# Rows of the targets' terms by 32x32 transposes on VectorE behind one small product, and edge counts in 16 bits

## The reference

```python
h = (x @ W).reshape(n, H, C)
alpha_s = jnp.einsum('nhc,hc->nh', h, a_s)
alpha_d = jnp.einsum('nhc,hc->nh', h, a_d)
e = jax.nn.leaky_relu(alpha_s[src] + alpha_d[dst], 0.2)
m = jax.ops.segment_max(e, dst, num_segments=n)
e = jnp.exp(e - m[dst])
denom = jax.ops.segment_sum(e, dst, num_segments=n)
alpha = e / (denom[dst] + 1e-16)
out = jax.ops.segment_sum(h[src] * alpha[:, :, None], dst, num_segments=n)
...
out = layernorm(x + gat(elu(gat(x, 8 heads) + b1), 1 head) + b2)
```

## Time and profile before

| | us |
|---|---|
| median of 3 runs | 641.88 (641.84 to 642.15) |
| profiled execution | 641.79 |
| its span | 640.0 |
| TensorE busy | 632.6 |
| VectorE busy | 529.6 |
| ScalarE busy | 336.3 |
| GpSimd busy | 208.1 |

### The profile page before, as it was taken

One profiled execution on the slowest core, in us unless ns is written; L12 is line 12 of the kernel. 1 busy time (PEld: TensorE's weight loads), 2 busy tenths in 40 slices (PEclk: granted clock), 3 DMA queues, 4 the chain that ended last, 5 costly groups with the idle time before them and its releaser, 6 DMA issues.

```text
span 640.0 us, 9306 instructions
## 1 busy us (share of the span) xinstructions
PE 632.6 (99%) x3426; PEld 543.9 (85%) x3426; DVE 529.6 (83%) x928; ACT 336.3 (53%) x570; POOL 208.1 (33%) x122
## 2 busy tenths in 40 slices
PE   9999999999999999999999999999999999999996
PEld 5766568989888898989899988999898989887885
DVE  8999997889989878758684858797689868789876
ACT  7899982546524645444353635363455344534382
POOL 1000000140743824067404940375207540451230
PEclk9999999999999999999999999999999999999999
DMA  8422503125144323042302520270307130500002
GB/s 317 161 75 75 160 15 99 50 54 194 51 147 146 127 99 99 1 153 95 100 1 72 175 59 16 75 227 23 97 20 237 65 100 5 192 26 1 1 2 99
DMA packets 22173, 59.36 MB, mean 93 GB/s; under 512 B 2544, under 2 KB 2800, under 8 KB 22128
## 3 DMA queue, kind: packets, MB, share of 16 engines
q1 hardware_dynamic: 21984, 58.69, 28.2%
q10 hardware_dynamic: 144, 0.07, 0.0%
HBM read 54.03 MB, written 4.72 MB: 92 GB/s over the span
## 4 chain that ended last, share of the span: by engine, by line
PE 89%; DVE 9%; issue 0%; ACT 0%; DMA 0%; ACTq 0%
PE O L1289 31%; PE R L1184 9%; PE R L1190 9%; PE R L1187 9%; PE R L1256 6%; PE R L1262 6%; PE R L1259 6%; DVE ohd L709 3%; PE O L1201 3%; DVE ohs L713 2%; PE R L1206 1%; DVE junk L749 1%; PE O L1256 1%; PE O L1262 1%; PE O L1259 1%; PE O L1434 1%
## 5 line engine op out<-in xcount | busy, mean ns | idle before, releaser
L1111 POOL TENSOR_TENSOR W2l<-Wr,W2h 128x768 fp32r<-128x768 f32 x48 | 92.6, 1948 | 126.1 <-ACT W2h L425 126.1
L1184 PE MATMUL R<-W1h,xTh 128*128 128x384 f32 x312 | 106.3, 341 | 0.0
L1115 POOL TENSOR_TENSOR Pl<-L,Ph 128x512 fp32r<-128x512 f32 x34 | 55.5, 1651 | 153.8 <-ACT Ph L474 153.6
L1187 PE MATMUL R<-W1l,xTh 128*128 128x384 f32 x312 | 105.4, 338 | 0.0
L1190 PE MATMUL R<-W1h,xTl 128*128 128x384 f32 x312 | 105.4, 338 | 0.0
L1105 POOL TENSOR_TENSOR W1l<-Wr,W1h 128x768 fp32r<-128x768 f32 x30 | 58.8, 1970 | 129.3 <-ACT W1h L414 128.9
L749 DVE CUSTOM_DVE_ANT_0 junk<-h,abc 128x768 bf16<-128x768 f32 x64 | 64.0, 999 | 27.8 <-ACT h L437 26.7
L1289 PE MATMUL O<-W2h,gh 128*128 128x256 f32 (+1 forms) x384 | 78.5, 339 | 0.0
L1289 PE MATMUL O<-W2h,gl 128*128 128x256 f32 (+1 forms) x384 | 77.4, 336 | 0.0
L1289 PE MATMUL O<-W2l,gh 128*128 128x256 f32 (+1 forms) x384 | 77.4, 336 | 0.0
L1256 PE MATMUL R<-Ph,hh 128*128 128x512 f32 x168 | 66.3, 395 | 0.0
(11 more groups left out here) (186 smaller groups left out, 1186.2 us busy)
## 6 DMA issues: line engine op xcount, KB each, us to landing
Wr<-in_W SPq DMA_DIRECT2D x101, 384.0 KB, 3.6
abc<-in_as SPq DMA_DIRECT2D x9, 384.0 KB, 5.5
abc<-in_ad SPq DMA_DIRECT2D x9, 384.0 KB, 5.3
h_rows<-h SPq DMA_DIRECT2D x8, 384.0 KB, 2.4
hl<-h_rows SPq DMA_DIRECT2D x8, 384.0 KB, 6.0
xin<-in_xT SPq DMA_DIRECT2D x6, 256.0 KB, 5.8
xr<-in_x SPq DMA_DIRECT2D x1, 1536.0 KB, 6.7
out<-res SPq DMA_DIRECT2D x4, 384.0 KB, 2.3
```

The lines of the kernel that those rows point to most:

```text
L1111: e.tensor_tensor(W2l[:, m % N2, :], Wr[:, n, :], W2h[:, m % N2, :].bitcast(f32), ALU.subtract).then_inc(s_w2l, 1)
L1115: e.tensor_tensor(Pl[:, t, d0:d1], L[:, t, d0:d1], Ph[:, t, d0:d1].bitcast(f32), ALU.subtract).then_inc(s_Pl, 1)
L1184: e.matmul(bank[:, 0:HALF], xTh[:, f, xs], hi[:, ws], start=f == 0, stop=False)
L1187: e.matmul(bank[:, 0:HALF], xTh[:, f, xs], lo[:, ws], start=False, stop=False)
```

## The change

In heads 1 to 6 the two rows of the targets' terms are no longer made by eight transposes on TensorE. `terms` (VectorE) spreads the four columns of each quantity over 16 columns, masked by `quad` so that a partition keeps only the column of its own quarter. `columns` (TensorE) multiplies both (128 x 32) by `four`, which is one wherever two partitions agree modulo 32; each partition then has the 16 values of the partitions with its own number modulo 32. `rows` (VectorE) turns them by 32x32 transposes of a broadcast input into 512 columns: first `row2` in SBUF, for ScalarE, then the bank `r1`, for its own L814. The ring's use `r2` becomes `x`, released by `rows`. Heads 0 and 7 and the second layer keep the eight transposes. `terms(2)` moves from behind `maxima(2)` to behind `scale_A(1, 0)`. GpSimd builds `four` and `quad` at the start. `CT` becomes u16 in place of f32.

```diff
@@ RING
-    RING += [("r2", 2, 0), ("r1", 2, 0)]
+    RING += [("x", 2, 0), ("r1", 2, 0)]
...
-            RING += [("B", h, n) for n in range(4, 8)] + [("as", h, 0), ("r2", h, 0), ("r1", h, 0)]
+            RING += [("B", h, n) for n in range(4, 8)] + [("as", h, 0), ("x" if h < H - 1 else "r2", h, 0), ("r1", h, 0)]
...
-        CT = sb("CT", [128, NT, N], f32)
+        CT = sb("CT", [128, NT, N], u16)
...
+            if kind == "x":
+                return s_row, 2 * h
@@ ScalarE, scores
-                            e.wait_ge(s_bc, bc)
+                            if 0 < h < H - 1:
+                                e.wait_ge(s_row, 2 * h - 1)
+                            else:
+                                e.wait_ge(s_bc, bc_value(h, 1))
@@ VectorE, terms
+                if turned:
+                    if h == 1:
+                        e.wait_ge(s_four, 11)
+                    e.tensor_tensor(adm[:, :, :], by_b(ad), by_t, ALU.mult).then_inc(s_adm, 1)
                 e.wait_ge(s_amx, NT * h + hi)
                 e.tensor_tensor(zm[:, lo:hi], amx[:, lo:hi], ad, ALU.add).then_inc(s_zm, 1)
                 e.wait_ge(s_zm, n // 2 + 1)
+                if turned:
+                    e.tensor_tensor(zmm[:, :, :], by_b(zm[:, :]), by_t, ALU.mult).then_inc(s_zmm, 1)
+                    e.wait_ge(s_zmm, h)
+                    e.scalar_tensor_tensor(
+                        out=mcm[:, :, :], in0=zmm[:, :, :], scalar=SLOPE, in1=zmm[:, :, :], op0=ALU.mult, op1=ALU.max).then_inc(s_mc, 1)
+                    e.wait_ge(s_mc, h + 1)
+                    e.wait_ge(s_adm, h)
+                    e.tensor_tensor(rm[:, 0, :, :], adm[:, :, :], mcm[:, :, :], ALU.subtract).then_inc(s_r12, 1)
+                    e.scalar_tensor_tensor(
+                        out=rm[:, 1, :, :], in0=adm[:, :, :], scalar=SLOPE, in1=mcm[:, :, :], op0=ALU.mult, op1=ALU.subtract).then_inc(s_r12, 1)
+                    return
@@ VectorE, rows (called first thing in scores, heads 1 to 6)
+                cols = ring_bank("x", h, 0)[:, 0:2 * NT * 4].rearrange("p (i c) -> p i c", i=2)
+                e.wait_ge(s_bc, bc_value(h, 1))
+                if h > 1:
+                    e.wait_ge(s_L, NT * h)
+                e.transpose(row2[:, :].rearrange("p (c j) -> p c j", j=32), cols[:, 1, :].unsqueeze(2).broadcast_to([128, NT * 4, 32])).then_inc(s_row, 1)
+                if h == 1:
+                    e.wait_ge(s_y, 2)
+                else:
+                    e.wait_ge(*released(RING[RING_AT["r1", h, 0] - 2]))
+                e.transpose(ring_bank("r1", h, 0)[:, :].rearrange("p (c j) -> p c j", j=32), cols[:, 0, :].unsqueeze(2).broadcast_to([128, NT * 4, 32])).then_inc(s_row, 1)
@@ VectorE, order
                     maxima(h, 0, NT, ring_bank("as", h, 0))
+                    terms(h, 0, NT)
...
                     for i, k in enumerate(V_SCORES.get(h, ())):
                         products_W2(k, 0 if i else 8 * h + 8)
-                    scores(h, h, 0, NT, ring_bank("r1", h, 0), 3 * h + 3)
+                    scores(h, h, 0, NT, ring_bank("r1", h, 0))
...
                     scale_A(h, c)
+                    if h == 1 and c == 0:
+                        terms(2, 0, NT)
@@ GpSimd
+            e.tensor_tensor(four[:, 0:32], idn[:, 0:32], idn[:, 32:64], ALU.add).then_inc(s_four, 1)
+            e.tensor_tensor(four[:, 32:64], idn[:, 64:96], idn[:, 96:128], ALU.add).then_inc(s_four, 1)
+            e.wait_ge(s_four, 2)
+            e.tensor_tensor(four[:, 64:96], four[:, 0:32], four[:, 32:64], ALU.add).then_inc(s_four, 1)
+            e.wait_ge(s_four, 3)
+            for q in (0, 1, 3):
+                e.tensor_copy(four[:, 32 * q:32 * q + 32], four[:, 64:96]).then_inc(s_four, 1)
+            e.memset(quad[:, :], 0.0).then_inc(s_four, 1)
+            e.wait_ge(s_four, 7)
+            for b in range(4):
+                e.memset(quad[32 * b:32 * b + 32, b:b + 1], 1.0).then_inc(s_four, 1)
@@ TensorE
+            def columns(h, bank):
+                e.wait_ge(s_r12, 2 * h + 2)
+                if h == 1:
+                    e.wait_ge(s_four, 6)
+                e.matmul(bank[:, 0:2 * NT * 4], four[:, :], rm[:, :, :, :].rearrange("p i t b -> p (i t b)"), start=True, stop=True).then_inc(s_bc, 1)
...
-                            e.wait_ge(*((s_y, 5), (s_y, 3), (s_y, 4), (s_y, 6), (s_L, 2 * NT), (s_lk, 2 * NT))[n])
+                            e.wait_ge(*((s_y, 5), (s_y, 3), (s_y, 4), (s_y, 6), (s_row, 2), (s_lk, 2 * NT))[n])
...
-                    e.wait_ge(s_y, 2)
-                    targets(1, 0, NT, (ring_bank("r2", 1, 0), ring_bank("r1", 1, 0)), 4)
+                    e.wait_ge(s_y, 1)
+                    columns(1, ring_bank("x", 1, 0))
...
-                    if c == (0 if h == 2 else 1 if h == H - 1 else 2) and h > 1:
+                    if c == 1 and h == H - 1:
                         targets(h, 0, NT, (None, None), 2 * h + 2)
+                    elif 1 < h < H - 1 and c == (0 if h == 2 else 2):
+                        columns(h, take("x", h, 0))
```

More of the change, by code:

```diff
@@ L79, in gat_resnorm_kernel @@
         xTl = sb("xTl", [128, FT, N], f32r)
-        CT = sb("CT", [128, NT, N], f32)
+        CT = sb("CT", [128, NT, N], u16)
+        row2 = sb("row2", [128, N], f32)
+        four = sb("four", [128, 128], f32)
+        quad = sb("quad", [128, 4], f32)
+        adm = sb("adm", [128, NT, 4], f32)
+        zmm = sb("zmm", [128, NT, 4], f32)
+        mcm = sb("mcm", [128, NT, 4], f32)
+        rm = sb("rm", [128, 2, NT, 4], f32)
+        sb("pad1", [128, 300], f32)
         with ExitStack() as c4:
@@ L207, in gat_resnorm_kernel @@
         s_dh, s_dl = sem("s_dh"), sem("s_dl")
+        s_four, s_adm, s_zmm, s_row = sem("s_four"), sem("s_adm"), sem("s_zmm"), sem("s_row")
         s_A, s_y, s_ex, s_em, s_g, s_gh, s_gl, s_C = (
@@ L216, in oh_value, with bc_value @@
             return (s_ohsa, ACT_J.index(j) + 1) if on_act(j) else (s_ohsd, DVE_J.index(j) + 1)
+        def bc_value(h, i):
+            return 1 + i if h == 0 else 2 * h + 2 + i if h < H - 1 else 2 * H + 3 * (h - H + 1) + i
         def Pl_value(h, t):
@@ L451, in scaled_as, with scores @@
                 e.mul(as02[:, :], asd[:, h % 2, 0, :], SLOPE).then_inc(s_as02, 1)
-            def scores(h, n, lo, hi, b2k, free, bc, between=None):
+            def scores(h, n, lo, hi, b2k, free, between=None):
                 d0, d1 = 128 * lo, 128 * hi
@@ L549, in head_2 @@
                     evict_B(2, 0, u // 2 - 1)
-            scores(0, 0, 0, NT, ring_bank("r2", 0, 0), (), 2, head_2)
+            scores(0, 0, 0, NT, ring_bank("r2", 0, 0), (), head_2)
             evict_B(2, 1, 0)
@@ L562, in head_2 @@
                             evict_B(2, 3, u // 2 - 1)
-                    scores(1, 1, 0, NT, ring_bank("r2", 1, 0), (gl_value(0, FT - 1), (s_g, FT)), 5, head_2)
+                    scores(1, 1, 0, NT, row2, (gl_value(0, FT - 1), (s_g, FT)), head_2)
                     high_sums(1)
@@ L576, in scalar_program @@
                     scaled_as(2, 24)
-                    scores(2, 2, 0, NT, ring_bank("r2", 2, 0), (gl_value(1, FT - 1), (s_g, 2 * FT)), 8, lambda u: high_w1(3, 3 + u) if u in (1, 2) else None)
+                    scores(2, 2, 0, NT, row2, (gl_value(1, FT - 1), (s_g, 2 * FT)), lambda u: high_w1(3, 3 + u) if u in (1, 2) else None)
                     high_h(2, 0)
@@ L603, in scalar_program @@
                     high_w2(h - 1, 5)
-                    scores(h, h, 0, NT, ring_bank("r2", h, 0), (gl_value(h - 1, FT - 1), (s_g, FT * h)), 3 * h + 2,
+                    scores(h, h, 0, NT, row2 if h < H - 1 else ring_bank("r2", h, 0), (gl_value(h - 1, FT - 1), (s_g, FT * h)),
                            lambda u, h=h: high_w1(h + 1, 1 + u) if h + 1 < H and 1 <= u <= 4 else None)
@@ L680, in scalar_program @@
             scaled_as(H, 65)
-            scores(H, H, 0, NT, ring_bank("r2", H, 0), (gl_value(H - 1, FT - 1), (s_g, FT * H)), 26, first_h2)
+            scores(H, H, 0, NT, ring_bank("r2", H, 0), (gl_value(H - 1, FT - 1), (s_g, FT * H)), first_h2)
             part_h2(2, 1, 3)
@@ L796, in maxima, with terms @@
                         accum_out=amx[:, t:t + 1]).then_inc(s_amx, 1)
+            def terms(h, lo, hi):
+                par = h % 2
+                ad = asd[:, par, 1, lo:hi]
+                n = 2 * h if h < H else 2 * H + lo
+                turned = 0 < h < H - 1
+                by_t, by_b = quad[:, :].unsqueeze(1).broadcast_to([128, NT, 4]), (lambda a: a.unsqueeze(2).broadcast_to([128, NT, 4]))
+                if turned:
+                    if h == 1:
+                        e.wait_ge(s_four, 11)
+                    e.tensor_tensor(adm[:, :, :], by_b(ad), by_t, ALU.mult).then_inc(s_adm, 1)
                 e.wait_ge(s_amx, NT * h + hi)
@@ L805, in maxima, with rows, scores @@
                     out=r12[:, 1, lo:hi], in0=ad, scalar=SLOPE, in1=mc[:, lo:hi], op0=ALU.mult, op1=ALU.subtract).then_inc(s_r12, 1)
-            def scores(h, n, lo, hi, b1k, bc):
```

(22 more changed lines are left out.)

8 lines of the change are left out of this document (3 added, 5 removed).

## The result

The kernel after takes 644.22 us (median, 643.89 to 647.19, 10 runs) where the kernel before took 641.98 beside it (641.74 to 642.20, 10 runs): ratio 1.0045, 95% interval 1.0033 to 1.0057. It is slower, by 2.24 us, where 2.3 were forecast.

A forecast was written before the change was run, and what follows sets the result against it. TensorE was taken to bound the kernel (busy 632.6 of 640.0 us), VectorE only from 20 to 80 us. -5.27 + 0.9 + 0.3 + 1.15 + 0.26 + 5.0 = +2.3 on 641.79 gave 644.1 us; range 640.0 to 648.5.

The forecast's parts named there:

- case (b): Rival: same stalls but milder, 3.0 us in heads 5 and 6, 0.3 in head 1; 640.7, no change; chance 0.20.
- Removed and added on TensorE: Heads 1 to 6: 48 transposes go, -5.27 us on the chain; six 32-column products come, +0.9 us.
- The transposes: VectorE's two 128x512 transposes to rows out of PSUM: 0.69 us each, between 0.42 and 1.2.
- Case (e): Rival: transposes stream at half rate, over 0.9 us each, 1 us more in five heads; 649 us; chance 0.14.
- Heads 5 and 6: Rows wait behind VectorE's four W2 products, making W1l late: TensorE stalls 2.5 us each, 5.0 together.
- Head 2: Transposes lie in VectorE's 1.65 us idle gap before its first L814, moved terms in another gap: no cost.
- Heads 3 and 4: L466 starts 0.4 us later, W1l follows: TensorE stalls 0.13 us each, 0.26 in all.
- The small terms and GpSimd: Six small VectorE instructions in `terms`: 0.35 us more, nothing for TensorE; up to 3.7 later if two wait for GpSimd.
- Head 1: VectorE is full, so the transposes delay the fourth L814: TensorE stalls 1.15 us (0.3 to 2).
- Start: GpSimd's build of `four` and `quad` slows VectorE's first one-hots: 0.3 us (0 to 0.8).
- Counts in 16 bits: Count additions on the VectorE-bound chain, 2.27 us a pair, already read strided 16-bit values: no gain in the sum.
- Case (d): Rival: count additions halve, two binding pairs, 2.3 us less, 641.8 us; chance 0.04.

The follow-up runs named there:

- the three experiments on heads 5 and 6: Changed kernel with old rows in heads 5 and 6: 640.94 us; with the second W2 block behind the scores: 639.89; with half of each W2 product: 641.05.
- The experiment: Changed kernel, but head 1 has its rows from TensorE's eight transposes as before: 643.83 us, ratio 1.0039.
- counts: Kernel before with only CT in 16 bits, plus 4096 bytes a partition of padding so later tiles keep their places: 641.92 us, ratio 0.9999.
- counts without padding: Kernel before with only CT in 16 bits and no unused tile, so all tiles behind CT lie 4096 bytes lower: 642.02 us, ratio 1.0001.
- semaphores: Kernel before with 16-bit CT and the change's four semaphores declared but not used: 641.98 us, ratio 1.0001.

## Why the prediction was right

The mechanism is the one that was forecast, and the three experiments on heads 5 and 6 show it. The median came 0.1 us from the forecast, and that closeness is luck: 0.5 us were not in the sum, and 0.2 too much at the start, 0.2 too much in heads 5 and 6 and 0.1 too much in head 1 make up for them. One sum of the prediction is off: the terms of case (b) add up to 640.4, not 640.7; nothing else rests on it but its border with the forecast.

- **Removed and added on TensorE**: -5.27 + 6 x 0.14 = -4.43, forecast -4.37. Taking the chain's 0.88 for eight transposes, and not eight times the duration that one instruction has alone, was the step that decided. The product of 32 columns sat where the 2-column one pointed.
- **The transposes**: 0.71 and 0.69, forecast 0.69. Case (e), half rate, is out. The Trainium skill (Vector Engine (DVE) Microarchitecture Reference, "3.8 The reshape front-end and per-opcode configuration") gives one element per cycle and lane, and the trace agrees: the same 0.69 as an elementwise pass over 512 columns.
- **Heads 5 and 6**: 2.5 and 2.3, forecast 2.5 each. The single times were off and cancelled. ScalarE's pass started at 422.07, not 422.95, and without its waits TensorE would have loaded for the last `W1l` at 432.27 - 2.5 = 429.8, not 430.58. The prediction took only head 5's own saving off the times of before, while the earlier heads had already moved everything: TensorE starts C(4) at 405.94 where it started at 406.76, 0.82 us sooner, and VectorE's maxima of head 5 are as much sooner. The last `W1l` ended 10.15 behind the pass, as said, at 432.22. That the first of the two waits (0.75) lay one `W1l` ahead of the last was not seen and changes nothing in the sum. The two experiments on the W2 products and the one that gives up these heads show the mechanism, not only the size. The clock drop behind head 6's wait (1.45 us) was not foreseen; it is not in the median.
- **Head 2**: its new rows cost nothing, as said; the stretch is 0.67 us shorter, the saving was put at 0.73.
- **Heads 3 and 4**: 5.1 - 4.8 = 0.3 us in two waits, forecast 0.26.
- **The small terms and GpSimd**: the 128x4 addition met GpSimd, as before, and took 1.87 us; the four behind it took 0.17 to 0.18 each, and the last ended at 280.18, 2.7 us ahead of TensorE's 282.89. The price of two further waits was not paid.
- **Head 1**: mis-sized in its parts. The wait for L873 was 0.88 (forecast 1.15), and one of 0.33 for a bank of the ring came to it, which the prediction put at nothing: it charged the longer terms (0.2) only to the start of the first score, and did not follow them through ScalarE's list, where they delay an eviction that TensorE needs. The two waits less the 0.73 saved are +0.5. The experiment gives +0.4, and its stretch of the chain +0.3; forecast +0.4. The parts give more than the stretch because B(2)'s slow products (below) and these waits overlap: where TensorE comes later by itself, it waits less; this is argued, not isolated.
- **Start**: 0.3 forecast, about 0.1 found. VectorE's first one-hot took 0.45 us beside GpSimd's build, started at 3.64, and 0.35 without; from its start to a later product with h it is 26.20 us against 26.10 (26.11 with the build behind the counting), and medians give the build 0.09. In the kernel with the second W2 block later, which has the build too, the one-hot started at 3.53, took 0.35, and the distance is 26.11: so in these traces the build costs 0.1 us or nothing. The other 0.11 of the profile's +0.21 is the moment when an input arrived (the first one-hot starts at 3.64, not 3.53). Kernels with the same work up to there reach the end of the counting between 79.71 and 80.13 us in their traces, so a single trace doesn't settle tenths here.
- **Counts in 16 bits**: nothing, as taken. Case (d) is out: two additions take 2.36 us as before.
- **Not in the sum**: the 0.5 us at B(2)'s products between 80 and 184 us (80 to 128 us takes 48.70 us and not 48.37, then to 184 us 55.87 and not 55.67). It lies in all kernels that have the change's code, also where no new instruction is executed before that point, and in the medians of none of the four that lack it (before, counts, counts without padding, semaphores). The width of the counts and the four semaphores are excluded. So is a shift of everything behind `CT` by 4096 bytes: the counts without padding have one step of 0.26 us at 117.1 us, 0.173 from there on, and 48.37 us from 80 to 128 us. What is left are the places of the small tiles and of the instructions; neither was tried alone, and the cause stays open.

So -4.43 + 0.1 + 1.21 + 0.3 + 4.8 + 0.5 = +2.5 by the parts, +2.3 without what head 1 counts twice, against +2.24 in the medians and about +2.4 in the profile without its clock drop and its input's arrival.

## What to carry to other kernels

Work taken off the busiest engine is worth its length on the chain, but only if its replacement stands early enough in its new engine's queue: here 4.4 us were saved, and 4.8 lost in the two heads where four products of about 1 us stood in front of a 0.7 us transpose. Before moving an operation to another engine, write down what is queued ahead of it there and follow the delay through the in-order programs behind it (pass, casts, `W1l`) to the instruction that waits. Then move what stands in front: putting one block of W2 (two of the four products) behind the scores turned a loss of 2.2 us into a gain of 2.0.

## What the runs showed of the hardware

- A 128x512 f32 transpose of 32x32 blocks out of PSUM with a broadcast input takes 0.71 us into SBUF and 0.69 into PSUM, where an elementwise pass over as many columns takes 0.69.
- A plain f32 product of 128x128 by 128x32 runs as two instructions and takes 0.14 us of the chain.
- After waits of 0.55 and 1.75 us, three products apart, the granted clock fell for 3.2 us (1.45 us lost) in the profiled execution; waits of 0.75 and 1.75 us, as far apart, in the same execution had no such effect. By the times, four of ten executions have a drop. When a wait of this size costs the clock too can't be told from these runs.
- Products of one shape with nothing between them follow every 0.173 or every 0.177 us in the same stretch, in different kernels, and the runs don't tell what sets it.
